# A window-graph convolution layer and an inverted-bottleneck layer on one core: the offset transpose moved up, two images per loop turn, one product moved to GpSimd

## The chip, the cores and the metric

The kernel runs on one core of a Trainium2 chip. The metric is the time of one execution on the device, in microseconds (us), as the median of the runs shown. The engines are TensorE (PE in the profile, PEld its weight loads), VectorE (DVE), ScalarE (ACT), GpSimd (POOL) and SyncE (SP), each with its own instruction stream; they are ordered against one another only by semaphores.

## The reference, cut to what matters

The input x has 16 images of 96 channels and 64 by 64 pixels. Two layers follow each other.

```python
# layer 0: windows of 8x8 = 64 nodes, K = 9 neighbours
y = affine(conv1x1(x, fc1_w, fc1_b), fc1_s, fc1_t)
nodes = window_partition(y, 8)                      # (B*64, 64 nodes, 96)
xn = nodes / max(norm(nodes), 1e-12)
dist = sq - 2 * xn @ xn.T + sq.T
idx = top_k(-dist, 9)
feat = concat(x_i, x_j - x_i)                       # x_j gathered by idx
h = max_k(gelu((feat @ ew.T + eb) * es + et))       # 192 channels
x = affine(conv1x1(window_reverse(h), fc2_w, fc2_b), fc2_s, fc2_t) + x
# layer 1: 96 -> 576 -> 96, depthwise 3x3
h = relu(bn(w1 @ x)); h = relu(bn(depthwise3x3(h, wd))); x = x + bn(w2 @ h)
```

## The kernel before

An image is worked off in 32 slots, one for each pair of windows (`PAIRS`), and a chunk is 4 pairs (8 rows of pixels). P is the number of a pair over all images, p its slot in the image. Both layers run interleaved: while the pairs of one image go through layer 0, layer 1 follows in strips of 16 rows, some slots behind. Every engine's stream is written by a function `image(b, p0, p1)` that issues the engine's share slot by slot; tables (`FC1_AT`, `XN_AT`, `TAP_AT` and so on) say in which slot each shared job falls. `image_loop` issues images -1 (half), 0, then 1 to 14 in a hardware loop (`Fori`), one image per turn, then 15 and 16 as straight code.

In slot P, TensorE computes the scores of pair P+3 (`scores`, L517), `gather(P, 0)` (L567, the gathered values of the first window by a product with a one-hot matrix), the first quarter of the shared jobs, `expand(P+1)` (L540), `feature_transpose(P+2)` (L530, the neighbour offsets of pair P+2 transposed into columns 256 to 319 of the PSUM bank `pself`), `gather(P, 1)`, the other shared jobs, `self_full(P)` (L581, which writes the same bank `pself`), `values(P+1)` (L554, into `pvu`), `gather(P, 2)` (L570) and `self_half(P)` (L587).

ScalarE follows: `gelu(P, 0)`, evacuations of the first jobs, `tap0`, `onehot(P+1)` (L741, two instructions), `featT_copy(P+2)` (L727), `gelu(P, 1)`, the other evacuations, `vu_copy(P+1)` (L749), `feature_square(P+3)` (L732), `gelu(P, 2)`, `gelu_self(P)` (L764), then late `tap0` (L774) and `relu2` (L781) work. `self_full` waits until `featT_copy` has read the bank:

```python
pe.wait_ge(featT_evac, P + 3 if not isinstance(P, int) else min(P + 3, NPAIRS))
```

VectorE does the depthwise taps (L949, about 5 in a slot, each `scalar_tensor_tensor` with two inputs from SBUF), the top 8 of the scores (L902), their indices (L909), `feature_a` (L919) and the maximum over neighbours (`maxima`, L936). In slots 11 to 14 and 27 to 30 of an image it also runs `normalise` (L930), xn = y times the inverse norms for one chunk of 97 by 512 values. GpSimd copies each such chunk to xs (`stationary_copy`, L403), computes the inverse norms in slots 7 and 23 (L385 to L395), and issues two kinds of accumulating DMAs (`add_input`, L361, and `add_x1`, L370). SyncE writes the inverse norms to DRAM and reads them back broadcast to all partitions (`broadcast_norms`, L314 to L322, slots 9 and 25); their landing is counted by `rows_loaded`. The scores of a chunk wait for its xs.

Of the kernel before, what the change touches and what calls it, by code (L numbers as in the profile page):

```python
# [4 lines left out]
B, C, H, W = 16, 96, 64, 64  # L5
# [7 lines left out]
CHUNKS = H // WS  # L13
# [13 lines left out]
def valid(v, n):  # L27

    return not isinstance(v, int) or 0 <= v < n
# [71 lines left out]
def part_of(jobs, part):  # L101

    return [k for k in range(len(jobs)) if sum(k >= f * len(jobs) for f in PART_STARTS) == part]
# [61 lines left out]
def due(count):  # L165

    return not isinstance(count, int) or count > 0


def build(nc, x, p97, p128, rows97, consts, consts128, consts16, out):  # L170
# [3 lines left out]
    with ctx:  # L174
# [106 lines left out]
        def image_loop(eng, image, tail):  # L281

            image(-1, 16, PAIRS)
            image(0, 0, PAIRS)
            with eng.Fori(1, B - 1) as b:
                image(b, 0, PAIRS)
            image(B - 1, 0, PAIRS)
            image(B, 0, tail)

# [61 lines left out]
        @block.gpsimd  # L351
        def _(pool):
            pool.wait_ge(consts_ready, 2)
            xv = x.rearrange("b c row col -> b c (row col)")
            x1v = x1[:, :, :].rearrange("c row col -> c (row col)")

            def add_input(b, p, bc, c):

                pool.wait_ge(misc_evac, job_at(b, p, "fc2", c))
                pool.sem_inc(pool_passed, 1)  # L360
                nc.gpsimd.dma_start(x1v[:, c * CW:(c + 1) * CW], xv[bc, :, c * CW:(c + 1) * CW],  # L361
                                    accum_op=ALU.add).then_inc(x1_sum[c % 4], 16)

            def add_x1(b, p, o, t, s, q):

                fb, fp = when(b, p, 1)
                pool.wait_ge(misc_evac, job_at(fb, fp, "w2", q))
                pool.sem_inc(pool_passed, 1)
                c = 2 * t + q // 2
                nc.gpsimd.dma_start(res[:, q // 2, :], x1v[:, c * CW:(c + 1) * CW],  # L370
                                    accum_op=ALU.add).then_inc(out_sum[q // 2], 16)

            def inverse_norms(b, p, bi, h):


                n = 2 * bi + h
                fb, fp = when(b, p, 1)
                if due(count := job_at(fb, fp, "ssq", 4 * h + 3)):
                    pool.wait_ge(misc_evac, count)

                if due(count := 32 * n):
                    pool.wait_ge(rows_loaded, count)
                pool.sem_inc(pool_passed, 1)
                inv = norms[:, 0, :]
                nc.gpsimd.tensor_scalar(clamped[:, :], ssq[:, :], 1e-24, None, ALU.max).then_inc(pool_step, 1)  # L385
                pool.wait_ge(pool_step, 4 * n + 1)
                nc.gpsimd.tensor_tensor(inv, clamped[:, :], expo[:, 0:1].to_broadcast([128, 4 * PPC]),
                                        ALU.pow).then_inc(pool_step, 1)
                pool.wait_ge(pool_step, 4 * n + 2)
                nc.gpsimd.tensor_tensor(sqn[:, 0, :], ssq[:, :], inv, ALU.mult).then_inc(pool_step, 1)  # L390
                pool.wait_ge(pool_step, 4 * n + 3)
                nc.gpsimd.tensor_tensor(sqn[:, 1, :], sqn[:, 0, :], inv, ALU.mult).then_inc(pool_step, 1)
                pool.wait_ge(pool_step, 4 * n + 4)
                pool.sem_inc(pool_passed, 1)
                nc.gpsimd.tensor_scalar(norms[:, 1, :], sqn[:, 1, :], -0.5, None, ALU.mult).then_inc(inv_ready, 1)  # L395

            def stationary_copy(bi, c):

                pool.wait_ge(xn_ready, CHUNKS * bi + c + 1)
                if due(count := PPC * (CHUNKS * bi + c - 3)):  # L400
                    pool.wait_ge(score_ready, count)
                pool.sem_inc(pool_passed, 1)
                nc.gpsimd.tensor_copy(xs[0:C, c % 4, :], xn[0:C, c % 4, :]).then_inc(xs_ready, 1)  # L403

            def image(b, p0, p1):
                for p in range(p0, p1):
                    h = 1 if p < 16 else 0
                    bi = b if h else b + 1
                    if p % 16 == NORMS_AT and valid(bi, B):
                        inverse_norms(b, p, bi, h)  # L410
                    for o, t, s, q in due_in(ADD_AT, b, p):
                        add_x1(b, p, o, t, s, q)
                    if p % 16 in XN_AT and valid(bi, B):
                        stationary_copy(bi, 4 * h + XN_AT[p % 16])
                    if p % 4 == 1:
                        bc, c = (b, (p - 5) // 4) if p >= 5 else (b - 1, CHUNKS - 1)
                        if valid(bc, B):
                            add_input(b, p, bc, c)

            image_loop(pool, image, TAIL)  # L420


        @block.tensor
        def _(pe):
# [97 lines left out]
            def feature_transpose(P, p):  # L522
                if due(count := P + 1):
                    pe.wait_ge(feat_ready, count)

                if due(count := P - 2):
                    pe.wait_ge(self_gelu, count)
                if due(count := P):
                    pe.wait_ge(featT_evac, count)
                nc.tensor.matmul(pself[:, 256:320], feat[:, p % 2, :], I2,  # L530
                                 start=True, stop=True).then_inc(featT_ready, 1)
# [61 lines left out]
            def image(b, p0, p1):  # L593
                for p in range(p0, p1):
                    P = PAIRS * b + p
                    if isinstance(b, int) and b == -1 and p == 16 + NORMS_AT:

                        pe.wait_ge(consts_ready, 2)
                    jobs = misc_jobs(b, p)
                    if valid(P + 3, NPAIRS):  # L600
                        scores(b, P + 3, p + 3)
                    if valid(P, NPAIRS):
                        if due(count := P + 1):
                            pe.wait_ge(onehot_ready, count)
                        if due(count := P + 1):
                            pe.wait_ge(vu_evac, count)
                        gather(P, p, 0)
                    for k in part_of(jobs, 0):
                        shared_job(b, p, k, jobs[k])
                    if valid(P + 1, NPAIRS):  # L610
                        expand(P + 1, p + 1)
                    if valid(P + 2, NPAIRS):
                        feature_transpose(P + 2, p + 2)
                    if valid(P, NPAIRS):
                        gather(P, p, 1)
                    for k in part_of(jobs, 1):
                        shared_job(b, p, k, jobs[k])
                    for k in part_of(jobs, 2) + part_of(jobs, 3):
                        shared_job(b, p, k, jobs[k])
                    if valid(P, NPAIRS):  # L620
                        self_full(P, p)
                    if valid(P + 1, NPAIRS):
                        values(P + 1, p + 1)
                    if valid(P, NPAIRS):
                        gather(P, p, 2)
                    if valid(P, NPAIRS):
                        self_half(P, p)
# [5 lines left out]
        def _(act):  # L633
# [156 lines left out]
            def image(b, p0, p1):  # L790
                for p in range(p0, p1):
# [6 lines left out]
                    bi = b if h else b + 1  # L798
                    if valid(P, NPAIRS):
                        gelu(P, p, 0)  # L800
                    for k in part_of(jobs, 0):
                        shared_evac(b, p, k, jobs[k])
                    for o, t, s, groups in due_in(TAP0_AT, b, p):
# [1 line left out]
                            tap0(b, p, o, t, gr)  # L805
                    if valid(P + 1, NPAIRS):
                        onehot(P + 1, p + 1)
                    if valid(P + 2, NPAIRS):
                        featT_copy(P + 2, p + 2)
                    if valid(P, NPAIRS):  # L810
                        gelu(P, p, 1)
                    for k in part_of(jobs, 1):
# [21 lines left out]
        def _(dve):  # L834
# [85 lines left out]
                                               in0=idx[:, r, :].unsqueeze(1).to_broadcast([128, 2, KN]),  # L920
                                               scalar=-32.0, in1=maskw, op0=ALU.add, op1=ALU.mult).then_inc(a_ready, 1)

            def normalise(b, p, bi, c):
                dve.wait_ge(rows_loaded, 32 * (2 * bi + c // 4 + 1))

                if due(count := PPC * (CHUNKS * bi + c - 3)):
                    dve.wait_ge(score_ready, count)
                if due(count := CHUNKS * bi + c - 3):
                    dve.wait_ge(xs_ready, count)
                nc.vector.tensor_tensor(xn[:, c % 4, :], y[:, c, :], invb[:, c % 4, :], ALU.mult).then_inc(xn_ready, 1)  # L930

            def maxima(P, p):
                c, j, r = (p % PAIRS) // PPC, p % PPC, p % 2
                if due(count := P + 1):
# [17 lines left out]
            def image(b, p0, p1):  # L952
                for p in range(p0, p1):
# [7 lines left out]
                        tap(*a)  # L961
                    if new:
                        largest(P + 3, p + 3)
                    if p % 16 in XN_AT and valid(bi, B):
                        normalise(b, p, bi, 4 * h + XN_AT[p % 16])
                    for a in taps[2:3]:
                        tap(*a)
                    if new:
# [96 lines left out]
```

## Time and profile before

| what | value |
|---|---|
| median of 3 runs | 4372.47 us (4371.74 to 4379.67) |
| the profiled execution | 4362.46 us, span 4360.7 us, mean granted TensorE clock 0.990 |
| busy: PE, PEld | 4041.2 us (93%), 2406.4 us (55%) |
| busy: DVE | 4081.9 us (94%) |
| busy: ACT | 3606.4 us (83%) |
| busy: POOL | 503.2 us (12%) |

The shares are of the span. The chain of waits is followed back from the last instruction, at each step to what released it. Idle time of an engine is listed with what ended it; "issue" is time in which an engine waited for nothing that the profile shows. Times of a window are us from the span's start.

### The profile page before, as it was taken

Reading aid. Unit: us, or ns where it says so; the run is one execution under the profiler, and the core shown is the slowest. Engines: PE = TensorE matmul, PEld = TensorE weight load, DVE = VectorE, ACT = ScalarE, POOL = GpSimd, SP = SyncE. Lnnn points to the kernel's source line nnn. Section 1 sums busy time; section 2 is a strip of 40 time slices with the busy share of each in tenths; the row PEclk is TensorE's granted clock in tenths of the full one; section 3 lists DMA queues with packets and bytes.
Section 4 is the critical chain, followed back from the end, with each engine's and each line's share of the span. In section 5 each row is a group of like instructions: output and inputs, shape, how many; then the busy total and the mean of one; then the engine's idle time right before and its main releaser. Section 6 shows DMA issues by size and latency. Waiting matters only on the chain.

```text
span 4360.7 us, 84229 instructions
## 1 busy us (share of the span) xinstructions
PE 4041.2 (93%) x26688; PEld 2406.4 (55%) x26688; DVE 4081.9 (94%) x5296; ACT 3606.4 (83%) x7141; POOL 503.2 (12%) x548
## 2 busy tenths in 40 slices
PE   4999999999999999999999999999999999999994
PEld 2555555555555555555555555555555555555552
DVE  2599999999999999999999999999999999999998
ACT  3788888888888888888888888888888888888883
POOL 0011111011111011011111010111010111010100
PEclk9999999999999999999999999999999999999997
DMA  1111120111111111121111111111111111201111
GB/s 47 23 30 32 25 45 18 33 38 32 33 30 28 29 36 34 25 44 19 33 36 33 33 26 24 37 33 33 30 33 25 38 32 25 45 18 25 30 21 24
DMA packets 53036, 134.61 MB, mean 31 GB/s; under 512 B 7778, under 2 KB 9058, under 8 KB 46372
## 3 DMA queue, kind: packets, MB, share of 16 engines
q0 software_dynamic: 28672, 50.35, 8.1%
q1 hardware_dynamic: 23876, 78.22, 6.7%
q8 instruction: 250, 4.10, 0.4%
q14 instruction: 238, 1.95, 0.2%
HBM read 77.68 MB, written 25.69 MB: 24 GB/s over the span
## 4 chain that ended last, share of the span: by engine, by line
PE 66%; issue 11%; DVE 11%; ACT 11%; DMA 0%; SPq 0%; ACTq 0%; DVEq 0%; POOL 0%; POOLq 0%
PE pg L567 15%; PE pmisc L493 8%; PE pg L570 8%; DVE acc L949 8%; PE pvu L554 7%; PE pmisc L477 5%; PE pself L581 5%; ACT MV L741 4%; PE pmisc L438 3%; PE pmisc L460 2%; PE pmisc L462 2%; PE pmisc L445 2%; PE pvu L540 2%; ACT hpad L688 2%; PE pmisc L495 2%
## 5 line engine op out<-in xcount | busy, mean ns | idle before, releaser
L949 DVE SCALAR_TENSOR_TENSOR acc<-hpad,w,acc 128x1024 f32<-128x1024 f32 (+1 forms) x2560 | 2919.5, 1174 | 66.1 <-ACT acc L774 66.1
L567 PE MATMUL pg<-MV,VU 128*128 128x512 f32 x2048 | 1148.0, 643 | 22.6 <-ACT VU L749 21.0
L758 ACT ACTIVATE g<-pg 128x512 f32<-128x512 f32 x1536 | 916.3, 597 | 147.5 <-PE pg L570 90.2
L936 DVE TENSOR_REDUCE hid<-g 128x192 f32<-128x1728 f32 x512 | 995.5, 1944 | 0.0
L741 ACT ACTIVATE MV<-pvu,cst 64x512 f32<-64x512 f32 x1024 | 694.8, 678 | 9.9 <-PE pvu L540 0.3
L477 PE MATMUL pmisc<-x,w 96*128 96x384 f32 (+1 forms) x1536 | 567.9, 481 | 18.4 <-ACT hpad L688 18.4
L570 PE MATMUL pg<-MV,VU 128*64 128x512 f32 x2048 | 530.3, 595 | 0.0
L493 PE MATMUL pmisc<-acc,w 128*96 128x256 f32 x2048 | 492.3, 384 | 31.3 <-ACT acc L781 31.3
L688 ACT ACTIVATE hpad<-pmisc,sh,sc 128x384 f32<-128x384 f32 (+1 forms) x768 | 482.4, 660 | 25.0 <-DVE acc L949 15.7
L477 PEld LDWEIGHTS pmisc<-x,w 96*128 96x128 f32 x1536 | 294.1, 192 | 326.0 <-issue 229.1
L581 PEld LDWEIGHTS pself<-MV,VU 128*128 128x128 f32 x2048 | 283.3, 191 | 335.7 <-issue 314.6
L493 PEld LDWEIGHTS pmisc<-acc,w 128*96 128x96 f32 x2048 | 334.8, 165 | 228.7 <-issue 122.5
L554 PE MATMUL pvu<-wVU,y 97*64 97x192 f32 x4096 | 447.9, 340 | 1.7 <-ACT MV L741 1.7
L581 PE MATMUL pself<-MV,VU 128*128 128x64 f32 x2048 | 308.3, 273 | 141.9 <-ACT featT L727 138.3
L749 ACT ACTIVATE VU<-pvu 128x384 f32<-128x384 f32 x512 | 250.9, 490 | 192.0 <-PE pvu L554 189.4
L781 ACT ACTIVATE acc<-acc,shd,scd 128x1024 f32<-128x1024 f32 (+1 forms) x320 | 358.0, 1142 | 24.4 <-DVE acc L949 24.4
L567 PEld LDWEIGHTS pg<-MV,VU 128*128 128x128 f32 x2048 | 309.4, 191 | 61.2 <-issue 30.4
L774 ACT ACTIVATE acc<-hpad,w 128x1024 f32<-128x1024 f32 (+1 forms) x320 | 334.2, 1044 | 0.0
L587 PEld LDWEIGHTS pself<-MV,VU 128*64 128x64 f32 x2048 | 145.4, 135 | 296.8 <-issue 296.8
L540 PEld LDWEIGHTS pvu<-featT,c 128*128 128x128 f16 x4096 | 186.0, 100 | 181.0 <-issue 156.5
L554 PEld LDWEIGHTS pvu<-wVU,y 97*64 97x64 f32 x4096 | 249.2, 136 | 55.6 <-ACT MV L741 2.0
L403 POOL COPY xs<-xn 96x512 f32<-96x512 f32 x128 | 159.5, 1247 | 1034.1 <-DVE xn L930 1034.1
(95 smaller groups left out, 4125.3 us busy)
## 6 DMA issues: line engine op xcount, KB each, us to landing
xin<-in_x_dram SPq DMA_DIRECT2D x32, 768.0 KB, 5.5
invb<-rows_dram SPq DMA_DIRECT2D x32, 768.0 KB
x<-in_x_dram POOLq DMA_DIRECT2D x128, 192.0 KB, 3.6
res<-x POOLq DMA_DIRECT2D x128, 192.0 KB, 3.6
out_dram<-res SPq DMA_DIRECT2D x128, 192.0 KB, 2.1
g<-in_consts_dram SPq DMA_DIRECT2D x1, 640.0 KB
w<-in_p_dram SPq DMA_DIRECT2D x1, 618.5 KB
rows_dram<-norm_rows SPq DMA_DIRECT2D x32, 16.0 KB, 1.4
```

Of the source, the lines that this page charges most:

```text
L477: last = nc.tensor.matmul(ps[:, o:o + (hi - lo) * W], w1T[:, gr * 128:(gr + 1) * 128], x1[:, lo:hi, :], start=True, stop=True)
L493: nc.tensor.matmul(ps[0:C, 0:4 * W], w2T[:, gr, :], acc[:, par, gr, q * 4 * W:(q + 1) * 4 * W], start=(gr == 0), stop=False)
L554: last = nc.tensor.matmul(pvu[h:h + 64, O * w:O * (w + 1)], nodes, wVU[:, k, :], start=True, stop=True)
L567: last = nc.tensor.matmul(ps[:, :], VU[:, r, part, 0:ONE128], cols[part], start=True, stop=True)
L570: last = nc.tensor.matmul(ps[64 * w:64 * w + 64, :], VU[:, r, w, ONE128:O], cols[w], start=True, stop=True)
L581: nc.tensor.matmul(pself[:, 64 * w:64 * w + 64], VU[:, r, w, 0:ONE128], MV[:, r, w, KN * NODES:], start=True, stop=True)
L688: nc.scalar.activation(hpad[:, gr, r0:r1, 1:W + 1], ps[:, o:o + (r1 - r0) * W].rearrange("p (row col) -> p row col", col=W), ACT.Relu, bia ...
L741: last = nc.scalar.activation(MV[h:h + 64, p % 2, w, 0:KN * NODES].rearrange("p (n k) -> p n k", k=KN), pone[h:h + 64, :, :].rearrange("p ...
L758: nc.scalar.activation(g[:, p % 2, part, :, 0:KN], pg[(3 * p + part) % 2][:, :].rearrange("p (n k) -> p n k", k=KN), ACT.Gelu).then_inc(ge ...
L781: nc.scalar.activation(acc[:, par, gr, 0:n], acc[:, par, gr, 0:n], ACT.Relu, bias=shd[:, gr:gr + 1], scale=scd[:, gr:gr + 1]).then_inc(rel ...
L936: nc.vector.tensor_reduce(hid[:, c % 2, j, :, :], g[:, r], op=ALU.max, axis=AX.X).then_inc(hid_ready, 1)
L949: nc.vector.scalar_tensor_tensor(out=dst, in0=src, scalar=wk, in1=dst, op0=ALU.mult, op1=ALU.add).then_inc(tap_done, 1)
```

## The change

Three edits. The transpose of the offsets (PE) goes right behind `gather(P, 0)` and its copy (ACT) right behind `gelu(P, 0)`, both ahead of the first shared jobs. The hardware loop takes two images per turn, 7 turns in place of 14. `normalise` goes from VectorE to GpSimd, right ahead of the copy of the same chunk, with the same waits.

```diff
-            with eng.Fori(1, B - 1) as b:
+            with eng.Fori(1, B - 2, 2) as b:
                 image(b, 0, PAIRS)
+                image(b + 1, 0, PAIRS)
...
+            def normalise(bi, c):
+
+                pool.wait_ge(rows_loaded, 32 * (2 * bi + c // 4 + 1))
+                pool.sem_inc(pool_passed, 1)
+                if due(count := PPC * (CHUNKS * bi + c - 3)):
+                    pool.wait_ge(score_ready, count)
+                pool.sem_inc(pool_passed, 1)
+                if due(count := CHUNKS * bi + c - 3):
+                    pool.wait_ge(xs_ready, count)
+                pool.sem_inc(pool_passed, 1)
+                nc.gpsimd.tensor_tensor(xn[:, c % 4, :], y[:, c, :], invb[:, c % 4, :], ALU.mult).then_inc(xn_ready, 1)
+
...
                     if p % 16 in XN_AT and valid(bi, B):
+                        normalise(bi, 4 * h + XN_AT[p % 16])
                         stationary_copy(bi, 4 * h + XN_AT[p % 16])
...
                         gather(P, p, 0)
+                    if valid(P + 2, NPAIRS):
+                        feature_transpose(P + 2, p + 2)
                     for k in part_of(jobs, 0):
                         shared_job(b, p, k, jobs[k])
                     if valid(P + 1, NPAIRS):
                         expand(P + 1, p + 1)
-                    if valid(P + 2, NPAIRS):
-                        feature_transpose(P + 2, p + 2)
...
                         gelu(P, p, 0)
+                    if valid(P + 2, NPAIRS):
+                        featT_copy(P + 2, p + 2)
...
                         onehot(P + 1, p + 1)
-                    if valid(P + 2, NPAIRS):
-                        featT_copy(P + 2, p + 2)
...
-            def normalise(b, p, bi, c):
-                dve.wait_ge(rows_loaded, 32 * (2 * bi + c // 4 + 1))
-
-                if due(count := PPC * (CHUNKS * bi + c - 3)):
-                    dve.wait_ge(score_ready, count)
-                if due(count := CHUNKS * bi + c - 3):
-                    dve.wait_ge(xs_ready, count)
-                nc.vector.tensor_tensor(xn[:, c % 4, :], y[:, c, :], invb[:, c % 4, :], ALU.mult).then_inc(xn_ready, 1)
-
...
-                    if p % 16 in XN_AT and valid(bi, B):
-                        normalise(b, p, bi, 4 * h + XN_AT[p % 16])
```

## Rows read from the trace of the kernel before

**Rows 1.** The page, part 4: the chain that ended last, by engine.
```profile
PE 66%; issue 11%; DVE 11%; ACT 11%; DMA 0%; SPq 0%; ACTq 0%; DVEq 0%; POOL 0%; POOLq 0%
```

**Rows 2.** Windows of images 1, 7: us; busy PE, PEld, DVE, ACT, POOL; clock; DMA.
```profile
307.45:567.64 260.19, 248.95 (x1661) 148.77 (x1659) 253.58 (x329) 224.46 (x447) 31.54 (x34) 1.00 0.16 32
...
1881.74:2144.22 262.48, 250.13 (x1668) 149.51 (x1668) 253.73 (x329) 224.69 (x447) 31.54 (x34) 1.00 0.16 32
```

**Rows 3.** Waits of PE in image 7: us in total, times, longest.
```profile
PE pself L581 <- ACT featT L727: 7.8, 12, 1.4
PE pscore L517 <- issue: 2.1, 1, 2.1
```

**Rows 4.** Waits of DVE in image 7.
```profile
DVE top L902 <- PE pscore L519: 4.9, 4, 1.5
DVE acc L949 <- ACT acc L774: 3.8, 3, 1.4
```

**Rows 5.** Window of slot 11 of image 7 (columns as in Rows 2).
```profile
1973.35:1981.60 8.25, 6.88 (x48) 3.42 (x46) 8.25 (x11) 7.79 (x16) 1.40 (x1) 1.00 0.00 1
```

**Rows 6.** The chain in slot 14 of image 7: start, us, what.
```profile
2002.36 0.68 ACT MV L741
...
2003.07 0.23 ACT featT L727
...
2003.43 0.63 PE pself L581 x4
```

**Rows 7.** Waits of PE over the whole span.
```profile
PE pself L581 <- ACT featT L727: 138.3, 200, 2.1
...
PE pscore L517 <- issue: 26.3, 13, 2.3
```

**Rows 8.** Waits of PE in slots 11 to 15 of image 7.
```profile
PE pself L581 <- ACT featT L727: 4.0, 4, 1.4
```

**Rows 9.** The timeline of PE and ACT around the start of slot 27 of image 7.
```profile
2103.09 1.13 PE L567 MATMUL pg<-MV,VU 128*128 128x512 f32 x2
2103.43 0.51 ACT L764 ACTIVATE g<-pself 128x192 f32<-128x192 f32 x1
```

**Rows 10.** The timeline of DVE in slot 11 of image 7: start, us.
```profile
1976.95 0.67 DVE L930 TENSOR_TENSOR xn<-y,invb 97x512 f32<-97x512 f32 x1
1977.54 1.28 DVE L949 SCALAR_TENSOR_TENSOR acc<-hpad,w,acc 128x1024 f32<-128x1024 f32 x1
...
1978.81 0.23 DVE L909 FIND_INDEX8 idx<-top,pscore 128x8 uint32<-128x64 f32 x1
1978.95 1.42 DVE L949 SCALAR_TENSOR_TENSOR acc<-hpad,w,acc 128x1024 f32<-128x1024 f32 x1
```

**Rows 11.** The timeline of POOL in slots 9 to 11 of image 7.
```profile
1962.15 0.79 POOL L361 DMA_DIRECT2D x<-in_x_dram  x1 [4.54 <-ACT x L671]
1977.89 1.40 POOL L403 COPY xs<-xn 96x512 f32<-96x512 f32 x1 [14.95 <-DVE xn L930]
```

**Rows 12.** Lines L403 and L392: ns min/median/max, first and last start us.
```profile
L403 POOL COPY xs<-xn x128: 599/1412/1478, 66.1 to 4106.8; 96x512 f32<-96x512 f32 x128
...
L392 POOL TENSOR_TENSOR sqn<-sqn,norms x32: 220/221/1249, 56.6 to 4045.2; 128x16 f32<-128x16 f32 x32
```

**Rows 13.** The timelines of POOL and DVE at 68.7 us.
```profile
68.67 0.61 POOL L403 COPY xs<-xn 96x512 f32<-96x512 f32 x1 [1.17 <-DVE xn L930]
...
68.75 0.56 DVE L919 SCALAR_TENSOR_TENSOR feat<-idx,cst 128x16 f16<-128x16 uint32 x1
```

**Rows 14.** The timeline of DVE in slots 9 and 10 of image 7.
```profile
1962.85 3.14 DVE L949 SCALAR_TENSOR_TENSOR acc<-hpad,w,acc 128x1024 f32<-128x1024 f32 x3
1967.35 1.28 DVE L949 SCALAR_TENSOR_TENSOR acc<-hpad,w,acc 128x1024 f32<-128x1024 f32 x1 [1.37 <-ACT acc L774]
...
1971.28 0.17 DVE L919 SCALAR_TENSOR_TENSOR feat<-idx,cst 128x16 f16<-128x16 uint32 x1
```

**Rows 15.** The queue of SP: the second load of the broadcast norms.
```profile
1954.58 0.28 SPq L322 DMA_DIRECT2D invb<-rows_dram  x1
```

## The prediction

> **What bounds the kernel now.** I read the chain of waits first. Two thirds of it are TensorE, and VectorE, ScalarE and plain issue time share the rest at 11% each [rows 1]: no engine bounds alone. Then one image in a window. Image 7 takes 262.48 us; PE is busy for 250.13 of them and DVE for 253.73 [rows 2]. So PE is idle for 12.35 us and DVE for 8.75. The reader should see that the two are almost equally full, so that a gain on one is worth only what the other's idle time leaves room for. The waits say where that idle time lies. PE waits 7.8 us, in 12 slots of 32, at `self_full` for the copy of the offsets; and 2.1 us once, at the loop turn [rows 3]. DVE waits 4.9 us for scores and 3.8 us for tap 0 [rows 4]. The slots in which PE waits for the copy are mostly those in which DVE has no gap: in slot 11, DVE is busy for all 8.25 us, PE for 6.88 [rows 5]. This decides what the first edit can bring.
>
> **Edit 1, the transpose and its copy moved up.** Before, PE's `self_full` cannot start until ACT has done `onehot` and, behind it, the copy of 0.23 us; then come the 0.63 us of `self_full` [rows 6], and only then `values`. After it, the copy is done ahead of `onehot`, so `self_full` runs while `onehot` does, and `values` waits for `onehot` alone. The copy still costs ACT its 0.23 us ahead of `values`; what leaves the path is `self_full`, at most 0.63 us in a slot, and no more than PE's wait there. Over the whole span there are 200 such waits, 138.3 us, 0.69 us on average [rows 7]. In image 7 the 12 waits are 7.8 us; four of them, in slots 11 to 15, are together 4.0 us [rows 8]. Capped at 0.63 us, those four, 1.0 us on average, lose some 1.5 us; with as much lost in their twins of the second half, at most, the 12 give some 5 us. In slots 11 and 27 ACT has work without a gap up to `vu_copy` (busy 7.79 of 8.25 us in slot 11 [rows 5]), so that an earlier `values` releases nobody; without their 1.3 us, 3.9 us an image at most are left. Most of that falls where DVE is full. I take 40%, 1.6 us an image and 26 us over 16 images, because PE's lead can be used only up to the next place where DVE idles for scores. Ends: nothing, and 3.9 x 16 = 62 us.
>
> What the edit may cost: on PE the transpose now waits, behind `gather(P, 0)`, for `gelu_self(P-1)`, which reads the same bank; behind it are queued the first jobs, `expand` and `gather(P, 1)`. At the start of slot 27, `gelu_self` ends at 2103.94 and `gather(P, 0)` at 2104.22 [rows 9]: 0.28 us to spare, cost nothing. If DVE delivers `feature_a` late, then ACT's `feature_square`, `gelu(P-1, 2)` and `gelu_self` come late in turn, and PE is held where it could have done jobs before. In slots in which ACT does late tap 0 or `relu2` work behind `gelu_self`, ahead of `onehot`, that is covered. I count zero.
>
> **Edit 2, the loop turn.** PE idles 26.3 us in 13 waits on "issue" ahead of the first scores of an image [rows 7], 2.02 us a turn. Image 1, which is entered from straight code, takes 2.3 us less than image 7 [rows 2]. Of 13 jumps back, 6 stay; 7 x 2.02 = 14 us go. Ends: 7 x 2.3 = 16 us, and zero, if DVE's work hides it. The Trainium skill (Runtime: NRT & Kernel Launch, "Instruction fetch mechanics") states that a taken branch to a target outside the fetched pages stalls until that page has been fetched, while straight code streams; the trace agrees with its one stall at each turn.
>
> **Edit 3, `normalise` on GpSimd: what it removes.** On DVE a `normalise` takes 0.59 us from start to next start (1976.95 to 1977.54 [rows 10]). The copy behind it also costs DVE something: it starts at 1977.89, while a tap is running, and takes 1.40 us [rows 11] although a copy alone takes 0.60 [rows 12]; so it waited for the tap's end at 1978.82. The tap after that takes 1.42 us in place of 1.28 [rows 10]: 0.14 us lost, with `indices` in between covering about 0.29. So a copy blocks a two-input instruction of DVE for 0.14 + 0.29 = 0.43 us. At 68.67 a copy met `feature_a` with nothing in between: 0.56 us [rows 13] in place of 0.17 [rows 14], a loss of 0.39. DVE and POOL exclude each other. Even products of 16 values on POOL take 221 ns as a rule and 1249 at most [rows 12], when they queue behind a tap. The removal is 8 x (0.59 + 0.14) = 5.8 us an image.
>
> **What it adds.** A product of 512 values with two SBUF inputs on POOL is not in the trace. From below: a copy's block, 0.43 us. From above: twice a whole copy, 1.2 us. It reads two streams where the copy reads one, so I take twice 0.43, about 0.9 us of block. The Trainium skill (GPSIMD Engine Reference, "Performance versus the Vector engine") gives 4497 ns for such an instruction at 2048 values and rates it about two times slower than on VectorE, a rule that speaks against this edit; a quarter of it, an estimate from that page, is 1.12 us. The Trainium skill (SBUF — State Buffer, "SBUF: two separate sides") says that the loser of the shared port pair is blocked for the whole instruction; the copy's 0.43 us of 0.60 says a little less. By the page's figure the sum below would be some 25 us worse.
>
> Where it falls: POOL no longer waits for DVE's turn in slot 11. The norms' load is issued by 1954.86 [rows 15], and POOL is free at 1962.94 after `add_input` [rows 11]. No row shows the landing; I take it that 8 us are enough, and if not, the gap named next is missed, as in rival 1. POOL then runs product, copy, product, copy, product, copy for three chunks in a row, from slot 9 on. DVE is then in three taps (3.14 us) and, after them, idle for 1.37 us until tap 0 comes [rows 14]: the first product and copy, 0.9 + 0.43, vanish in that gap. The other four fall between taps: 0.8, 0.3 (behind it `largest`, which is not blocked), 0.6 (behind it `indices`) and 0.43, together 2.1 us. The fourth chunk has to wait for `add_input` and `add_x1` of slots 13 and 14, and costs about 0.7 + 0.4. That is 3.2 us per half image against 2.9 removed: +0.3, or +0.6 an image, +10 us in all. From the slot 10 on which DVE is on the chain, 2.1 us come before slot 11 gives its 0.73 back, so it is a delay before it is a relief. Behind the waiting POOL instructions are the two kinds of DMAs; POOL idled 14.95 us ahead of its first copy [rows 11], and its chunks are ready slots before the scores of slot 13, so nobody waits for POOL.
>
> **Sum.** -14 (turns) - 26 (transpose) + 10 (GpSimd) = -30 us. Against the profiled execution of 4362.46 us that gives 4332; the median of the runs shown is 10 us above that execution, so 4372.47 - 30 = 4342 us.
>
> **Rivals.**
> 1. *The exclusion of DVE and POOL becomes the bound; slower.* Place: the taps of slots 9 to 11, 14 and their twins. Were the block 1.2 us, seven of eight products an image cost 0.3 more, 34 us; were the phase such that the 1.37 us gaps are not used, 2.7 us an image, 43 us more; and if DVE's fullness left the first edit nothing, 26 more. All three make 4445; the first two, 4419. The sign turns at 30 us, a block of about 1.15 us at an unchanged phase. For it: DVE is the fuller engine and has no gap in just these slots. Against it: DVE leads the chain only in a few slots.
> 2. *DVE's relief counts in full; much faster.* The block is nearer 0.43 us or falls under `maxima`, which reads one input. Then 0.47 x 6 x 16 = 45 us come on top: 4297, and with all of the first edit 4261. For it: from slot 11 on DVE is full, and PE has over 1 us a slot to catch up.
> 3. *Nothing.* The exclusion eats the 30 us, or the transpose's early wait for `gelu_self` gives back what `self_full` gained: 4372.
>
> **Chances and range.** The forecast (4310 to 4363): 0.42; rival 2: 0.17; rival 3: 0.13; rival 1: 0.28. A measurement of this kernel can tell about 0.2% from no change, 9 us. Faster 0.59, same 0.13, slower 0.28. The range reaches into rivals 1 and 2, with half of each outside: 4275 to 4405. The forecast's own is 4310 to 4363.
>
> **What would show it.** Right: the wait of L581 for L727 nearly gone, with `values` waiting for L741 at less than before; 6 issue waits at the scores in place of 13; POOL's product at 1 us or more when alone and up to 2.3 behind a tap; taps right behind a POOL instruction longer by 0.3 to 0.9 us; DVE busy about 255 to 257 us an image. Wrong: products that block over 1.1 us, a wait of PE at L530 for `gelu_self`, or of ACT's L732 for DVE, growing beyond 1 us in slots 10 and 28; or an image below 258 us.

## The result, and the profile after

The changed kernel takes 4412.5 us (median of 4 runs, 4407.45 to 4419.26) against 4373.11 us for the kernel before: the ratio is 1.0093, 95% interval 1.0078 to 1.0108. It is 0.9% slower, outside the range of the prediction. The profiled execution of the changed kernel took 4410.42 us, its span is 4408.7 us.

The page of the kernel after first: the busy times, then the chain that ended last, by engine (its counterpart is [rows 1]).

```profile
PE 4117.9 (93%) x26688; PEld 2434.4 (55%) x26688; DVE 4167.6 (95%) x5168; ACT 3613.1 (82%) x7141; POOL 663.8 (15%) x676
...
PE 55%; DVE 20%; issue 15%; ACT 8%; DVEq 1%; DMA 0%; SPq 0%; ACTq 0%; POOL 0%; POOLq 0%
```

Two things are to be seen. VectorE does 128 instructions fewer and is busy for 85.7 us more (4081.9 before), and its share of the chain went from 11% to 20%. And TensorE, whose instructions are the same in number and kind, is busy for 76.7 us more (4041.2 before). For the first the forecast had a smaller rise, to 255 to 257 us an image (259.68 in the image below); for the second it had no cause.

Next, a window of image 7 of the kernel after (columns as in [rows 2]): its slot 10, then the whole image.

```profile
1987.73:1996.92 9.19, 7.07 (x46) 3.94 (x45) 9.19 (x9) 6.71 (x15) 5.10 (x4) 1.00 0.00 0
1901.96:2168.80 266.84, 255.19 (x1676) 151.14 (x1676) 259.68 (x321) 225.08 (x447) 42.30 (x42) 1.00 0.15 31
```

The same slot of the kernel before:

```profile
1966.42:1973.35 6.93, 6.65 (x46) 3.80 (x45) 6.00 (x9) 6.71 (x16) 0.00 (x0) 1.00 0.01 2
```

The image went from 262.48 to 266.84 us, and slot 10 alone from 6.93 to 9.19, in which DVE has no idle time left. The timelines of slots 9 and 10 show why; first POOL, then DVE.

```profile
1984.26 2.37 POOL L408 TENSOR_TENSOR xn<-y,invb 97x512 f32<-97x512 f32 x1
1986.83 0.81 POOL L416 COPY xs<-xn 96x512 f32<-96x512 f32 x1 [0.20 <-POOL xn L408]
1987.62 1.27 POOL L408 TENSOR_TENSOR xn<-y,invb 97x512 f32<-97x512 f32 x1
1989.08 1.36 POOL L416 COPY xs<-xn 96x512 f32<-96x512 f32 x1 [0.19 <-POOL xn L408]
1990.40 1.26 POOL L408 TENSOR_TENSOR xn<-y,invb 97x512 f32<-97x512 f32 x1
1991.86 1.36 POOL L416 COPY xs<-xn 96x512 f32<-96x512 f32 x1 [0.19 <-POOL xn L408]
```

```profile
1984.21 8.54 DVE L954 SCALAR_TENSOR_TENSOR acc<-hpad,w,acc 128x1024 f32<-128x1024 f32 x4
...
1992.81 1.48 DVE L954 SCALAR_TENSOR_TENSOR acc<-hpad,w,acc 128x1024 f32<-128x1024 f32 x1
```

The products of three chunks do run in a row from slot 9 on, as the prediction had it. But four taps take 8.54 us. In slot 21 of the kernel before, four take 4.33 (one of the four is 128x512 in both places):

```profile
2060.38 4.33 DVE L949 SCALAR_TENSOR_TENSOR acc<-hpad,w,acc 128x1024 f32<-128x1024 f32 x4
```

The product lasts 1.27 us when it has the ports at once. And a copy that gets them is followed by the product of the next chunk within its own last moments (1987.62 against a copy that ends at 1987.64): the tap that waits for the copy waits for the product as well.

The waits of TensorE over the whole span of the kernel after, against [rows 7]:

```profile
PE pg L581 <- ACT VU L763: 35.0, 60, 0.8
PE pscore L531 <- DVE idx L923: 34.8, 30, 1.7
PE pself L544 <- ACT feat L746: 32.6, 31, 1.6
...
PE pvu L568 <- ACT MV L755: 28.0, 79, 1.5
...
PE pscore L531 <- issue: 12.4, 6, 2.3
```

The 138.3 us at `self_full` are gone, with 28.0 us at `values` in their place, and of 13 waits at the loop turn 6 are left, as forecast. New are 34.8 us of waits for VectorE's indices and 32.6 us at the transpose. The profile puts these down to `feature_square` (L746). But all of them except the first two of the run end 0.10 us behind the end of `gelu_self` (L778), as in image 7 right behind slot 10:

```profile
1996.41 0.51 ACT L778 ACTIVATE g<-pself 128x192 f32<-128x192 f32 x1
...
1997.02 0.19 PE L544 MATMUL pself<-c,feat 128*128 128x64 f16 x1 [1.03 <-ACT feat L746]
```

So does every one of the 33 waits there that the profile gives to "issue" (14.3 us). The transpose waits for `gelu_self`, 44.2 us in 62 waits.

### The profile page after: what moved, and what is told of

Same layout as the page of the kernel before. It is cut to its first block, busy times and chain, and to the rows that moved or that the text cites. A ratio compares the mean times of both kernels' runs of the same rounds, so it can differ in the third digit from the quotient of the medians.

```text
span 4408.7 us, 84265 instructions
## 1 busy us (share of the span) xinstructions
PE 4117.9 (93%) x26688; PEld 2434.4 (55%) x26688; DVE 4167.6 (95%) x5168; ACT 3613.1 (82%) x7141; POOL 663.8 (15%) x676
## 4 chain that ended last, share of the span: by engine, by line
PE 55%; DVE 20%; issue 15%; ACT 8%; DVEq 1%; DMA 0%; SPq 0%; ACTq 0%; POOL 0%; POOLq 0%
DVE acc L954 16%; PE pg L581 13%; PE pmisc L507 8%; PE pg L584 6%; PE pvu L568 6%; PE pmisc L491 4%; PE pmisc L452 3%; PE pmisc L459 3%; DVE hid L941 2%; ACT MV L755 2%; PE pself L595 2%; PE pmisc L474 2%; PE pmisc L509 2%; PE pmisc L476 2%; PE pvu L554 1%
## 5 line engine op out<-in xcount | busy, mean ns | idle before, releaser
L954 DVE SCALAR_TENSOR_TENSOR acc<-hpad,w,acc 128x1024 f32<-128x1024 f32 (+1 forms) x2560 | 3085.4, 1244 | 13.9 <-ACT acc L788 13.9
L491 PE MATMUL pmisc<-x,w 96*128 96x384 f32 (+1 forms) x1536 | 590.9, 497 | 22.9 <-ACT hpad L702 17.2
L362 POOL DMA_DIRECT2D x<-in_x_dram x128 | 102.8, 803 | 2299.7 <-ACT x L685 2000.6
L491 PEld LDWEIGHTS pmisc<-x,w 96*128 96x128 f32 x1536 | 284.7, 194 | 272.0 <-issue 169.1
L595 PEld LDWEIGHTS pself<-MV,VU 128*128 128x128 f32 x2048 | 304.9, 191 | 117.9 <-issue 55.4
L371 POOL DMA_DIRECT2D res<-x x128 | 104.9, 819 | 1247.1 <-ACT res L733 1193.0
L595 PE MATMUL pself<-MV,VU 128*128 128x64 f32 x2048 | 291.2, 265 | 0.0
```

The lines of the kernel that those rows point to most:

```text
L491: last = nc.tensor.matmul(ps[:, o:o + (hi - lo) * W], w1T[:, gr * 128:(gr + 1) * 128], x1[:, lo:hi, :], start=True, stop=True)
L595: nc.tensor.matmul(pself[:, 64 * w:64 * w + 64], VU[:, r, w, 0:ONE128], MV[:, r, w, KN * NODES:], start=True, stop=True)
L954: nc.vector.scalar_tensor_tensor(out=dst, in0=src, scalar=wk, in1=dst, op0=ALU.mult, op1=ALU.add).then_inc(tap_done, 1)
```

## The experiments

All times are medians. The kernel before took 4365 to 4371 us beside them and 4373 beside the changed kernel, so a difference between runs of different groups is more exact by their ratios. Theory A: the loss is the exclusion of VectorE and GpSimd. Theory B: it is what the moved transpose costs TensorE.

### Each part alone

`e1_loop` is the first hunk of the change alone.

```diff
-            with eng.Fori(1, B - 1) as b:
+            with eng.Fori(1, B - 2, 2) as b:
                 image(b, 0, PAIRS)
+                image(b + 1, 0, PAIRS)
```

> The kernel before with two images per loop turn and nothing else. Both theories expect 7 of the 13 waits on issue of 2.0 us to go: 14 us less, ratio 0.9968, with 6 such waits left in the profile. If VectorE's work hides the turn, the ratio is 1.000.

Measured: 4349.16 us, ratio 0.9951 (0.9937 to 0.9965), 21 us less. The waits on issue went from 26.3 us to this row of it:

```profile
PE pscore L518 <- issue: 12.4, 6, 2.3
```

That is 13.9 us less, and the interval of the ratio begins at 15 us. The gain is a little larger than the waits removed; what the rest is stays open.

`e2_transpose` is the move in `image` of TensorE and of ScalarE alone.

```diff
                         gather(P, p, 0)
+                    if valid(P + 2, NPAIRS):
+                        feature_transpose(P + 2, p + 2)
...
                         expand(P + 1, p + 1)
-                    if valid(P + 2, NPAIRS):
-                        feature_transpose(P + 2, p + 2)
...
                         gelu(P, p, 0)
+                    if valid(P + 2, NPAIRS):
+                        featT_copy(P + 2, p + 2)
...
                         onehot(P + 1, p + 1)
-                    if valid(P + 2, NPAIRS):
-                        featT_copy(P + 2, p + 2)
```

> The kernel before with the transpose of the offsets and its copy moved up and nothing else. Theory A (the loss of the whole change is the exclusion of VectorE and GpSimd): 10 to 26 us less than before, ratio 0.994 to 0.998. Theory B (the transpose behind the wait for gelu_self costs TensorE some 0.14 us a slot, as the profile after shows with 77 us more busy time): the time goes up by 10 to 50 us, ratio 1.002 to 1.011, and PE's time from the start of the transpose to the next product is 0.1 to 0.2 us in the median in place of 0.03.

Measured: 4382.44 us, ratio 1.0026 (1.0015 to 1.0037), 11 us more, where 26 us less had been predicted. PE is busy for 4100.7 us, 59.5 more than before. From the start of the transpose to the next product it takes 0.13 us in the median over the slots, in place of 0.03. That is theory B's side, though the small sum said nothing yet of its parts. TensorE also waits at the transpose here, 80 times, 32.9 us in all, each time until 0.10 us behind the end of `gelu_self`.

`e3_normalise` is the move of `normalise` alone.

```diff
+                        normalise(bi, 4 * h + XN_AT[p % 16])
                         stationary_copy(bi, 4 * h + XN_AT[p % 16])
...
-                    if p % 16 in XN_AT and valid(bi, B):
-                        normalise(b, p, bi, 4 * h + XN_AT[p % 16])
```

> The kernel before with normalise on GpSimd and nothing else. Theory A: 50 to 70 us more, ratio 1.011 to 1.016, with taps of up to 2.9 us in slots 9 and 10. Theory B: the exclusion is mostly absorbed by the idle time of VectorE; at most 20 us more, ratio up to 1.005.

Measured: 4470.88 us, ratio 1.023 (1.0216 to 1.0244), 100 us more: more than twice what the whole change costs, and more than theory A had. TensorE's waits in this run:

```profile
PE pself L594 <- ACT featT L740: 153.6, 198, 2.3
PE pscore L530 <- DVE idx L922: 32.3, 30, 1.1
```

Its slots 11 to 13 of image 7 (columns as in [rows 2]; slot 11 before is in [rows 5]), and then slots 12 and 13 of the kernel before:

```profile
2029.32:2038.54 9.22, 6.85 (x36) 3.71 (x37) 9.22 (x12) 8.04 (x17) 0.00 (x0) 0.81 0.00 1
2038.54:2047.34 8.80, 8.24 (x55) 4.57 (x54) 8.80 (x11) 7.76 (x17) 0.00 (x0) 1.00 0.00 0
2047.34:2055.80 8.46, 8.46 (x56) 5.35 (x55) 8.46 (x12) 6.74 (x13) 2.81 (x3) 1.00 0.26 36
```

```profile
1981.60:1990.40 8.80, 7.57 (x54) 4.56 (x54) 8.80 (x12) 7.76 (x16) 1.42 (x1) 1.00 0.00 0
1990.40:1998.85 8.45, 8.45 (x56) 5.37 (x56) 8.45 (x11) 6.72 (x13) 2.95 (x3) 1.00 0.24 36
```

Two things stand here. VectorE has no `normalise` in slots 12 to 14 any more, and they are as long as before (slot 14 takes 7.93 us in both): its relief is worth nothing there. And slot 11 is longer, with a lower granted clock. In image 7 TensorE waits 2.27 us for the copy of the offsets, and behind that wait the granted clock falls to 0.50, that is 1.2 GHz in place of 2.4. First the wait, then a window from the part at the lower clock:

```profile
2034.05 0.63 PE L594 MATMUL pself<-MV,VU 128*128 128x64 f32 x4 [2.27 <-ACT featT L740]
```

```profile
2035.50:2037.50 2.00, 2.00 (x12) 0.72 (x9) 2.00 (x3) 0.91 (x3) 0.00 (x0) 0.50 0.00 0
```

At a clock of 1.00, slots 11 and 27 take 8.25 us in this run as in the kernel before. Over images 1 to 14, those of them with a lower clock sum to 31 us above that length, against 2 us in the kernel before. So an estimated 29 of the 100 us are the clock's.

`e4_loop_transpose` is the changed kernel with `normalise` back on VectorE; from the changed kernel:

```diff
-                        normalise(bi, 4 * h + XN_AT[p % 16])
                         stationary_copy(bi, 4 * h + XN_AT[p % 16])
...
+                    if p % 16 in XN_AT and valid(bi, B):
+                        normalise(b, p, bi, 4 * h + XN_AT[p % 16])
```

> The changed kernel with normalise back on VectorE: loop and transpose alone. Theory A: 24 to 40 us less than before, ratio 0.991 to 0.9945. Theory B: 5 us less to 35 us more, ratio 0.999 to 1.008.

Measured: 4355.58 us, ratio 0.9969 (0.9957 to 0.9981), between the two ranges. The two parts add up within the noise: -21 + 11 = -10, measured -15. So in the changed kernel `normalise` on GpSimd costs 4412.5 - 4355.6 = 57 us (54 by the ratios), and both theories hold something.

`e12_norm_transpose` completes the square; from the changed kernel:

```diff
-            with eng.Fori(1, B - 2, 2) as b:
+            with eng.Fori(1, B - 1) as b:
                 image(b, 0, PAIRS)
-                image(b + 1, 0, PAIRS)
```

> normalise on GpSimd and the transpose as in the changed kernel, the loop as before. Alone they cost 100 and 11 us; if they add up, 111 us more, ratio 1.0256. If the earlier copy shortens the way that opens behind a late VectorE in slots 11 and 27 (TensorE waited there 2.3 and 2.2 us for the copy in the run with normalise alone): 50 to 75 us more, ratio 1.011 to 1.017.

Measured: 4439.42 us, ratio 1.017 (1.0154 to 1.0187), 75 us more where the sum of the parts is 111. The two edits do interact, by 36 us in the kernel's favour, and this hides part of what `normalise` costs in the changed kernel. Two things show in the profiles. With the earlier copy, e3's waits at `self_full` are gone, and slots 11 and 27 with a lower clock are 14 us above their length at full clock, in place of 31: some 15 of the 36 us. And VectorE's relief counts: against `e2_transpose`, slot 13 of image 7 is 0.36 us shorter and slot 14 is 0.50 (7.21 us against 7.71). First slot 13 of e2, then of this run:

```profile
1996.46:2005.51 9.05, 8.67 (x56) 5.33 (x55) 9.05 (x12) 6.72 (x13) 2.95 (x3) 1.00 0.23 32
```

```profile
2023.68:2032.37 8.69, 8.66 (x56) 5.33 (x55) 8.69 (x11) 6.71 (x13) 2.81 (x3) 1.00 0.23 33
```

### Why the transpose costs

Two explanations of e2's busy time were open: the early wait (theory W), or a small 16-bit product between 32-bit ones (theory P). `e5_wait` adds the wait alone; the transpose stays where it was.

```diff
                         gather(P, p, 0)
+                    if valid(P + 2, NPAIRS) and due(count := P):
+                        pe.wait_ge(self_gelu, count)
```

> The kernel before, with one more wait in TensorE's stream: behind gather(P, 0), for gelu_self(P-1), with the transpose where it was. Theory W (the early wait is what costs: TensorE's sequencer can no longer run ahead of the product in progress, and what it issues next comes late): 10 to 50 us more, ratio 1.002 to 1.011. Theory P (it is the small 16-bit product between two 32-bit ones, behind which the next weights are not loaded in time, whoever waits): 3 us more at most, ratio up to 1.001.

Measured: 4424.86 us, ratio 1.0129 (1.0114 to 1.0145), 56 us more, from one added wait and nothing else. `e11_wait_met` has the same wait for a signal of the slot before, long met; from `e5_wait`:

```diff
-                    if valid(P + 2, NPAIRS) and due(count := P):
+                    if valid(P + 2, NPAIRS) and due(count := P - 1):
                         pe.wait_ge(self_gelu, count)
```

> The kernel before with the same additional wait instruction behind gather(P, 0) as in the run that lost 56 us, but for gelu_self of the pair before the last, which has long been done. If it is the late signal that costs: ratio 0.999 to 1.001. If a wait instruction at that place costs by itself: ratio 1.003 or above.

Measured: 4366.89 us, ratio 1.0008 (0.9999 to 1.0017). So it is the signal that comes late, not the wait instruction. In it the weight load of the same job is 0.43 us ahead of the product again, as without the wait:

```profile
1930.62 0.95 PE L445 MATMUL pmisc<-ones,ysq 96*128 96x1 f32 x8
...
1930.19 0.19 PEld L445 LDWEIGHTS pmisc<-ones,ysq 96*128 96x128 f32 x1 [0.24 <-issue]
```

The timelines at the start of slot 5 of image 7 show how a late signal costs. The kernel before, `gather(P, 0)`, the first job and its first weight load:

```profile
1924.71 1.13 PE L567 MATMUL pg<-MV,VU 128*128 128x512 f32 x2
1925.67 0.95 PE L445 MATMUL pmisc<-ones,ysq 96*128 96x1 f32 x8
...
1925.25 0.19 PEld L445 LDWEIGHTS pmisc<-ones,ysq 96*128 96x128 f32 x1 [0.24 <-issue]
```

The same place in `e5_wait`, with the last `gelu_self` on ScalarE (its end is 1957.26 + 0.52):

```profile
1956.91 1.12 PE L567 MATMUL pg<-MV,VU 128*128 128x512 f32 x2
1957.99 1.05 PE L445 MATMUL pmisc<-ones,ysq 96*128 96x1 f32 x8
...
1957.99 0.97 PEld L445 LDWEIGHTS pmisc<-ones,ysq 96*128 96x128 f32 x8 [0.78 <-issue]
...
1957.26 0.52 ACT L766 ACTIVATE g<-pself 128x192 f32<-128x192 f32 x1
```

And in the kernel after, where the transpose L544 stands there:

```profile
1945.53 1.12 PE L581 MATMUL pg<-MV,VU 128*128 128x512 f32 x2
1946.50 0.19 PE L544 MATMUL pself<-c,feat 128*128 128x64 f16 x1
1946.70 1.05 PE L459 MATMUL pmisc<-ones,ysq 96*128 96x1 f32 x8
...
1946.47 0.10 PEld L544 LDWEIGHTS pself<-c,feat 128*128 128x128 f16 x1 [0.64 <-issue]
1946.69 0.97 PEld L459 LDWEIGHTS pmisc<-ones,ysq 96*128 96x128 f32 x8
```

Before, the first weights of the job are loaded 0.42 us ahead of its first product, while the 512 columns of `gather` still stream. With the wait, the load starts with the product, at 1957.99, and the job starts 1.08 us behind `gather`'s start in place of 0.96; its eight products take 1.05 us in place of 0.95. The signal came (1957.78) while the product in progress had still some 0.25 us to run; it was in time for the data and late for the weights. Over all slots the start of the next product behind `gather`'s start is 1.09 us in the median in `e5_wait` and 0.96 in the kernel before. In the kernel after, the load of the job starts with its product too, and the job begins 1.17 us behind `gather`. There the small product stands between as well, and what it adds (theory P) was not measured by itself. The Trainium skill (TensorE: Matmul & The Clock Gate, "Architectural detail: the array is 16× 32×32, not 1× 128×128") states that PE's queue can pull weight loads ahead of products in flight; these rows agree, and add that it cannot do so across a wait that is not yet met.

`e6_before_expand` keeps the idea and moves the wait away from that place: the transpose goes behind the first jobs.

```diff
                     for k in part_of(jobs, 0):
                         shared_job(b, p, k, jobs[k])
+                    if valid(P + 2, NPAIRS):
+                        feature_transpose(P + 2, p + 2)
                     if valid(P + 1, NPAIRS):
                         expand(P + 1, p + 1)
...
+                    if valid(P + 2, NPAIRS):
+                        featT_copy(P + 2, p + 2)
                     if valid(P + 1, NPAIRS):
                         onehot(P + 1, p + 1)
```

> The kernel before with the transpose right ahead of expand (behind the first jobs) on TensorE, and its copy right ahead of onehot on ScalarE: self_full is released as early as in the changed kernel, but the wait for gelu_self lies behind the first jobs and the product stands beside the other 16-bit ones. If the edit's gain is real and its cost only the place: 20 to 50 us less than before, ratio 0.989 to 0.995. If an earlier self_full is worth nothing because VectorE is full: ratio 0.999 to 1.001.

Measured: 4316.5 us, ratio 0.9883 (0.9868 to 0.9898), 52 us less, with PE busy for 4018.6 us. The idea is worth 52 us, and the place it was given in the change costs 63 us (against e2), more than all of it.

### Why the product on GpSimd costs

`e8_product_for_copy` leaves `normalise` on VectorE and makes GpSimd's copy a product.

```diff
-                nc.gpsimd.tensor_copy(xs[0:C, c % 4, :], xn[0:C, c % 4, :]).then_inc(xs_ready, 1)
+                nc.gpsimd.tensor_tensor(xs[0:C, c % 4, :], y[0:C, c, :], invb[0:C, c % 4, :], ALU.mult).then_inc(xs_ready, 1)
```

(SyncE's and ScalarE's waits for `xn_ready`, ahead of new norms and new y, are for `xs_ready` in it.)

> The kernel before with VectorE doing normalise as ever, and GpSimd computing xs as the product y times the inverse norms in place of the copy of xn: as many GpSimd instructions as before, at the same places, each a product. It measures what a product blocks against a copy (0.43 us). A block of 1.1 us makes the tap behind it 1.28 + 0.8 us long in place of 1.42, on VectorE 0.7 us more in 8 slots of an image; if these slots have slack there, 0 to 20 us more in all, ratio 1.000 to 1.005; if not, 60 to 90 us, ratio 1.014 to 1.021.

Measured: 4438.02 us, ratio 1.0163 (1.0149 to 1.0177), 70 us more. Its rows in slot 11 answer to [rows 10]; first POOL, then DVE:

```profile
2013.21 2.06 POOL L403 TENSOR_TENSOR xs<-y,invb 96x512 f32<-96x512 f32 x1 [14.95 <-DVE xn L930]
```

```profile
2014.12 0.23 DVE L909 FIND_INDEX8 idx<-top,pscore 128x8 uint32<-128x64 f32 x1
2014.26 2.10 DVE L949 SCALAR_TENSOR_TENSOR acc<-hpad,w,acc 128x1024 f32<-128x1024 f32 x1
```

The tap takes 2.10 us, in place of 1.28 alone and 1.42 behind a copy. By the reckoning of the prediction, a product blocks for 0.82 + 0.29 = 1.11 us, not 0.9. DVE is busy for 84 us more in all (4165.9 against 4081.9), and 70 us arrive in the time. In image 7, slots 11 to 14 take 8.91, 8.80, 8.94 and 9.02 us, in place of 8.25, 8.80, 8.45 and 7.93. So slots 11, 13 and 14 have no slack for a later VectorE, slot 12 has some; and with the transpose in its old place slots 12 to 14 gain nothing from an earlier one (e3).

`e7_norm_held` moves `normalise` to GpSimd but holds each chunk to its old slot.

```diff
+                if due(count := P + 4):
+                    pool.wait_ge(top8_ready, count)
```

> normalise on GpSimd, loop and transpose as before, but each chunk held until VectorE has done the top 8 of its old slot (a wait for top8_ready). Theory place (the 100 us of normalise on GpSimd come from where the products fall: in a row in slots 9 and 10, where VectorE sets the end): 0 to 40 us more than before, ratio 1.000 to 1.009, and slots 10 and 26 as long as before. Theory block (each product costs VectorE over 1 us wherever it falls): 70 us or more, ratio 1.016 or more.

Measured: 4414.46 us, ratio 1.0108 (1.0093 to 1.0124), 46 us more: between the two ranges. POOL and DVE in slot 11:

```profile
2002.94 1.70 POOL L410 TENSOR_TENSOR xn<-y,invb 97x512 f32<-97x512 f32 x1 [14.71 <-DVE top L918]
2004.84 1.35 POOL L418 COPY xs<-xn 96x512 f32<-96x512 f32 x1 [0.20 <-POOL xn L410]
```

```profile
2003.63 2.09 DVE L956 SCALAR_TENSOR_TENSOR acc<-hpad,w,acc 128x1024 f32<-128x1024 f32 x1
2005.64 0.57 DVE L935 SCALAR_TENSOR_TENSOR feat<-idx,cst 128x16 f16<-128x16 uint32 x1
```

Here the product costs a tap 0.81 us and the copy costs `feature_a` 0.40, against 0.59 + 0.14 removed: +0.48 us a chunk, 61 us over 128, an estimate from this one chunk; VectorE's busy time rose by 55.7 us (to 4137.6), and 46 show in the time. Where the products fall decides the other half of e3's 100 us: in the old slots 46, in a row in slots 9 and 10 another 54. Of these, VectorE's longer busy time (4172.5 us in e3) can give up to 35; and the lower clock is some 27 (31 us in slots 11 and 27, against 4 here). The two may overlap.

### What can be kept

`e9_loop_before_expand` is e1 and e6 together; `e10_after_before_expand` is the changed kernel with the transpose placed as in e6. From the changed kernel, on TensorE (`featT_copy` on ScalarE likewise, ahead of `onehot`):

```diff
                         gather(P, p, 0)
-                    if valid(P + 2, NPAIRS):
-                        feature_transpose(P + 2, p + 2)
                     for k in part_of(jobs, 0):
                         shared_job(b, p, k, jobs[k])
+                    if valid(P + 2, NPAIRS):
+                        feature_transpose(P + 2, p + 2)
                     if valid(P + 1, NPAIRS):
```

> Two images per loop turn, and the transpose right ahead of expand as in the run that gained 52 us; normalise on VectorE. If the two gains add up: 0.9951 x 0.9883 = 0.983, some 73 us less than before. If VectorE, busy for 95% in the second of them, is now the bound: no more than 60 us less, ratio 0.986 or above.

Measured: 4302.02 us, ratio 0.986 (0.9845 to 0.9876), 63 us less; the sum of the parts is 73, ratio 0.983, outside the interval. So they do not add up in full, as the second expectation had it; that VectorE is what stops them is not shown. It is the fastest kernel of the study.

> The changed kernel with only the transpose put right ahead of expand (and its copy right ahead of onehot): the same loop, normalise on GpSimd. Theory W (the place of the transpose costs the change some 60 us): 50 to 65 us less than the changed kernel, ratio 0.995 to 0.998 to the kernel before. If VectorE with its blocked taps sets the changed kernel's time alone: as the changed kernel, ratio 1.007 to 1.010.

Measured: 4363.19 us, ratio 1.000 (0.9991 to 1.0009). With this one move the changed kernel is as fast as the one before. By the ratios it is 41 us faster than it was (49 by the medians of the two groups), less than the 50 to 65 expected, and the ratio is 0.002, or 9 us, above the expected range: with `normalise` on GpSimd the better place is worth less than the 63 us between e2 and e6. Against e9, `normalise` on GpSimd costs 61 us here.

## Why the prediction was wrong

The forecast was wrong in sign, by 71 us. Some 25 of them are edits 1 and 2 together (-15 measured, -40 predicted) and some 44 to 47 are edit 3 (+54 to +57 measured, +10 predicted). Its first rival, at 28%, named the mechanism of the larger part, and its third that of the smaller: the transpose's early wait for `gelu_self`.

- **What bounds the kernel.** "The two are almost equally full" held. The text charged what edit 3 adds and what it removes at the same full rate. For what is added this was about right: in e8 70 of 84 us came through. For what is removed it was not: in e3 slots 12 to 14 are as long as before, and only with edit 1 (e12) do slots 13 and 14 become shorter.
- **Edit 2, the loop turn, -14 us.** Right in mechanism: 7 of 13 waits went. Measured -21 (interval from -15 to -28), more than its upper end of 16.
- **Edit 1, the gain, -26 us.** The idea was right and sized too small: in the place of e6 it brings 52 us. The 40% taken of 62 were a choice, not worked out, and the 3.9 us an image behind the 62 do not come out of the text's own terms (7.8 - 3.0 - 1.3 = 3.5).
- **Edit 1, the cost, "0.28 us to spare, cost nothing".** This step failed. It compared the end of `gelu_self` with the end of `gather(P, 0)`, that is with the time at which the next product could start. What the signal has to come in time for is the next weight load, 0.42 us ahead of that. e5 puts the wait by itself at 56 us; with the gain of 52, if the two add up, that makes +4 where e2 has +11. The text also took one slot for all: in e2 TensorE waits for the signal itself, with `gather` at its end, 80 times (32.9 us). The check that the text offered, a wait of more than 1 us at the transpose, came true in the kernel after (1.03 us in image 7, 44.2 us in all); what the missed weight loads cost shows in no wait, but in PE's busy time.
- **Edit 3, the block, "about 0.9 us".** Mis-sized: 1.11 us measured, a product alone 1.27. The estimate of 1.12 us from the page (the Trainium skill, GPSIMD Engine Reference, "Performance versus the Vector engine") is one of the whole product, and is 0.15 short of the 1.27 measured; that it meets the block of 1.11 is luck. At 1.12 the sum would still have been faster than before.
- **Edit 3, where it falls.** Slots 9 and 10, right. That each POOL instruction blocks one gap for itself was wrong: a tap that waits for a copy waits for the next product too, 0.43 + 1.11 = some 1.5 us at once. The 1.37 us gap did take in a part, as DVE has no idle time left in slot 10, but where the sum has +0.6 us an image, slot 10 of image 7 alone is 2.26 us longer, and the relief that was to pay for it came through in part only (0.36 + 0.50 us in slots 13 and 14 of image 7). DVE's busy time rose by 85.7 us in all. Predicted +10; measured +54 to +57 on top of the other two, +100 alone, of which an estimated 29 are the clock, a term that the prediction did not have.
- **The parts together.** The sum treated them as independent. The square of before, e2, e3 and e12 shows 36 us of interaction between edits 1 and 3, in the kernel's favour; without it the result would have been worse.

How the 54 us of e3 over e7 split between the double block, DVE's place on the chain and the clock was not tried; the figures above are read from one profile each.

## What to carry to other kernels

A wait on TensorE must be met not when the next product could start but when its weights could be loaded, here 0.42 us earlier; look at the start of the weight loads to see it, and try a late signal's wait behind the next jobs, as e6 does. Work moved from VectorE to GpSimd is not gone from VectorE if VectorE's next instruction reads two SBUF inputs, as the taps do: price it as nearly the whole duration on GpSimd (1.11 of 1.27 us for the product, 0.43 of 0.60 for the copy), and ask whether the slots that are relieved can become shorter at all. When an edit mixes a good idea with a bad place, run the idea alone in another place before the sum is judged: here that was worth 63 us, and 41 in the changed kernel.

## What the runs showed that was not expected

- A wait instruction that is met long before costs nothing that can be told (1.0008, 0.9999 to 1.0017); one that is met some 0.25 us ahead of the end of the product in progress costs 56 us over 512 slots, 0.11 us each.
- GpSimd, waiting with a copy and then a product, keeps VectorE's tap out for both: four taps took 8.54 us.
- TensorE's busy time is no fixed quantity of work: with the same 26688 products it was 4015.8 us in e9 and 4137.8 us in e5.
- A change of the other engines can lower TensorE's clock: in e3, 25 of the 28 slots 11 and 27 of images 1 to 14 had a granted clock of 0.71 to 0.88, and took up to 10.06 us in place of 8.25.
